# The ending of the last sequence pair moved into the slot that projects pair 0, and the first norm and small weight products into the last turn with heads or states

## What is computed

```
x = u
x = x + attn_a(layernorm(x), ...)   # selective state space block in chunk form (SSD)
x = x + ffn(layernorm(x), ...)      # two layers: local attention, then a gated feed forward
x = x + attn_b(layernorm(x), ...)   # a state scan over 256 steps, 16 states
x = x + ffn(layernorm(x), ...)      # the same two layers, the same weights
```

## Time and profile before

| | us |
|---|---|
| median of 3 runs | 2616.57 |
| lowest to highest | 2613.26 to 2620.62 |
| the profiled execution: its time | 2621.68 |
| the profiled execution: span of the trace | 2619.9 |
| TensorE busy | 2173.0 |
| VectorE busy | 1997.5 |
| ScalarE busy | 1836.2 |
| GpSimd busy | 1542.2 |

### The profile page before, as it was taken

One profiled execution on the slowest core, in us unless ns is written; L12 is line 12 of the kernel. 1 busy time (PEld: TensorE's weight loads), 2 busy tenths in 40 slices (PEclk: granted clock), 3 DMA queues, 4 the chain that ended last, 5 costly groups with the idle time before them and its releaser, 6 DMA issues. The chain is left out here.

```text
span 2619.9 us, 46190 instructions
## 1 busy us (share of the span) xinstructions
PE 2173.0 (83%) x13308; PEld 1114.0 (43%) x13308; DVE 1997.5 (76%) x5421; ACT 1836.2 (70%) x4729; POOL 1542.2 (59%) x1364
## 2 busy tenths in 40 slices
PE   5888689999999999666767667766799999999997
PEld 3555354555555555222222222222455555555553
DVE  4776477777777776389998999997777777777774
ACT  3444277777787777487787768875777777777774
POOL 1333275556565665176787777775756566665662
PEclk9998799999999999779899987989999999999999
DMA  3000000000000000000000000000000000000000
GB/s 130 1 0 1 5 18 9 14 13 9 13 14 13 12 9 14 0 0 1 1 1 1 0 1 1 0 0 1 14 17 10 12 14 10 13 18 21 17 14 17
DMA packets 12194, 29.92 MB, mean 11 GB/s; under 512 B 2240, under 2 KB 2240, under 8 KB 11584
## 3 DMA queue, kind: packets, MB, share of 16 engines
q1 hardware_dynamic: 11968, 27.41, 3.9%
HBM read 8.52 MB, written 2.10 MB: 4 GB/s over the span
## 5 line engine op out<-in xcount | busy, mean ns | idle before, releaser
L517 POOL TENSOR_TENSOR arena<-arena 128x512 f32<-128x512 f32 x256 | 325.1, 1270 | 447.0 <-DVE arena L1537 447.0
L573 POOL TENSOR_TENSOR arena<-arena 128x512 f32<-128x512 f32 x256 | 331.3, 1308 | 139.7 <-ACT arena L1262 137.2
L523 POOL TENSOR_TENSOR arena<-arena,SR 128x512 f32<-128x512 f32 x256 | 285.6, 1116 | 111.6 <-ACT SR L1144 110.7
L1617 DVE TENSOR_TENSOR_SCAN arena<-arena,psum 128x512 f32<-128x512 f32 x256 | 311.2, 1215 | 3.4
L935 PE MATMUL psum<-BS,tabs 96*128 96x512 bf16 x384 | 141.0, 424 | 194.0 <-DVE arena L1617 192.2
L1543 DVE TENSOR_REDUCE SM<-arena 128x8 f32<-128x512 f32 x256 | 175.6, 686 | 156.8 <-ACT arena L1134 143.8
L530 POOL TENSOR_TENSOR P<-P,RS 128x512 f32<-128x512 f32 x256 | 270.3, 1056 | 34.5 <-DVE RS L1464 34.1
L1003 PE MATMUL psum<-arena,first 128*128 128x512 f32 x512 | 288.7, 655 | 1.9 <-POOL arena L566 1.9
L1134 ACT ACTIVATE arena<-psum 128x512 f32<-128x512 f32 x256 | 151.6, 592 | 189.2 <-PE psum L859 187.9
L859 PE MATMUL psum<-rest,HA 128*128 128x512 f32 x512 | 270.4, 610 | 0.4 <-DVE HA L1452 0.4
L813 PE MATMUL psum<-HN,rest 128*128 128x512 f32 (+1 forms) x384 | 201.1, 651 | 56.1 <-ACT arena L1127 51.0
(11 more groups left out here) (221 smaller groups left out, 5237.4 us busy)
## 6 DMA issues: line engine op xcount, KB each, us to landing
arena<-arena SPq DMA_DIRECT2D x128, 128.0 KB, 2.3
rest<-in_rest SPq DMA_DIRECT2D x1, 4183.0 KB, 21.0
X<-in_x SPq DMA_DIRECT2D x1, 2048.0 KB, 9.0
out<-X SPq DMA_DIRECT2D x8, 256.0 KB, 2.3
tabs<-in_tabs SPq DMA_DIRECT2D x1, 1216.0 KB, 11.5
first<-in_first SPq DMA_DIRECT2D x1, 875.5 KB, 4.6
```

Source lines behind the costliest of these rows:

```text
L517: nc.gpsimd.tensor_tensor(CQ[:, n % 2, :], CQ[:, n % 2, :], SQN[:, n % 2, :], ALU.add).then_inc(f_rope, 1)
L523: nc.gpsimd.tensor_tensor(heads, heads, SR[:, n % 2, :].unsqueeze(2).to_broadcast([128, HEADS, DH]), ALU.mult).then_inc(f_qk, 1)
L573: nc.gpsimd.tensor_tensor(WU[:, k % DEEP, :], RG[:, k % DEEP, :], U[(t.j + pair) % 2][:, k % 2, :], ALU.mult).then_inc(m_wu, 1)
L1617: v.tensor_tensor_scan(HS[:, k % DEEP, :], AB[:, k % DEEP, :], B_BANK[k % 2], 0.0, ALU.mult, ALU.add).then_inc(m_hs, 1)
```

## The change

Four things are done, the arithmetic staying what it was.

1. Turn 8 is gone from both stages. VectorE still does its steps 0 and 1 right behind turn 7 (they finish the sum and gate it). The rest of pair 7's ending stands in slot -1, placed by tables from steps `h` of the slot to steps of the ending: `pe_closing`, `act_closing`, `dve_closing`. Its sums go to `CLOSE` (bank 1) in place of `STAT`.
2. The engines wait for `a_yd` and `m_g` (pair 7's sum is out of its banks) in place of `a_x` and `m_x` before the layers; `a_x` and `m_x` are waited for in slot -1 before the first scores.
3. Slot -2 is gone. Its contents, the first norm and shift of pair 0, stand in turn 7 (`t.final`) of each stage: in the scan the mean at `k` = 1, centring at 3, square at 5, variance at 7, root at 10, product and shift at 13.
4. The small weight products stand in turn 7 of the SSD stage: `small_sums` at steps 6 and 10 and the beta product at 11, the tables and biases on VectorE at 3, 5, 13 and 15.

```diff
+        CLOSE = bank[1]
...
         def passes(eng, ph, slot):
 
-            for n in (-2, -1, 0, 1):
+            for n in (-1, 0, 1):
                 slot(Slot(eng, ph, 0, n))
...
+                self.final = j == PAIRS - 1
+                self.stat = CLOSE if j == PAIRS else STAT
...
             turn(Turn(eng, 0, PAIRS - 1))
-            turn(Turn(eng, 0, PAIRS))
...
-            for j in range(PAIRS - 3, PAIRS + 1):
+            for j in range(PAIRS - 3, PAIRS):
                 turn(Turn(eng, 0, j))
...
+                    if t.final and q == 3:
+                        square_first(0)
...
+            staged(pool, pool_heads)
+            pool.wait_ge(a_yd, 2 * PAIRS)
             layers_pool(0)
...
+                    if t.final and k == 5:
+                        square_first(1)
...
+            def small_sums(l):
+                for g in range(2):
+                    for m, (at, size) in enumerate(HID_TILES):
+                        mm(X_BANK[1][0:size, 8 * l + 3 * g + m:8 * l + 3 * g + m + 1],
+                           W(f"w1{l}", HID * g + at, HID * g + at + size), W(f"lb{l}"), start=True, stop=True)
+
+            def a_pe_final(t, h):
+                first = Slot(pe, 0, 0, -2)
+                if h == 2:
+                    t.wait_ge(a_xt, 4, 4)
+                    pe.wait_ge(a_x, 1)
+                    outer_mean(first, X_BANK[0])
+                elif h in (6, 10):
+                    pe.wait_ge(in_rest, 16)
+                    small_sums((h - 6) // 4)
+                elif h == 8:
+                    outer_var(first, X_BANK[0])
+                elif h == 11:
+                    for k in range(2):
+                        last = mm(X_BANK[1][:, 16:17], W("b_wout", 128 * k, 128 * k + 128), W("b_beta", k, k + 1),
+                                  start=k == 0, stop=k == 1)
+                    last.then_inc(pre_ps, 1)
+
+            def pe_closing(k, h):
+                if k.ph:
+                    at = {3: 1, 4: 2, 8: 5, 9: 6, 15: 13, 16: 14}
+                    if h in at:
+                        pe_ending(Turn(pe, 0, PAIRS), at[h])
+                else:
+                    at = {5: 4, 6: 5, 13: 8, 14: 9}
+                    if h in at:
+                        a_pe_ending(Turn(pe, 0, PAIRS), at[h])
+
             def pe_dense(k, h):
+                if k.j == -1:
+                    pe_closing(k, h)
...
+                    if k.j == -1 and g == 6:
+                        pe.wait_ge(m_x if k.ph else a_x, PAIRS)
...
+                    if t.final and k == 1:
+                        t.wait_ge(m_zs, 2, 2)
+                        outer_mean(Slot(pe, 1, 0, -2), SIDE)
+                    if t.final and k == 7:
+                        outer_var(Slot(pe, 1, 0, -2), SIDE)
...
-            pe.wait_ge(m_x, PAIRS)
+            pe.wait_ge(m_g, 2 * PAIRS)
             layers_pe(1)
...
+            def act_closing(k, h):
+                if k.ph:
+                    at = {5: 7, 9: 10}
+                    if h in at:
+                        act_ending(Turn(act, 0, PAIRS), at[h])
+                else:
+                    at = {0: 2, 8: 6}
+                    if h in at:
+                        a_act_ending(Turn(act, 0, PAIRS), at[h])
...
+                    if t.final and k == 10:
+                        root_first(1, SIDE)
...
+            def a_dve_final(t, h):
+                if h == 3:
+                    dve.wait_ge(in_rest, 16)
+                    layer_tables(0)
+                elif h == 4:
+                    centre_first(0, X_BANK[0])
+                elif h == 5:
+                    layer_tables(1)
+                elif h == 12:
+                    normalise_first(0)
+                elif h == 13:
+                    dve.wait_ge(pre_ps, 1)
+                    layer_weights(0)
+                elif h == 15:
+                    layer_weights(1)
+                    scan_weights()
+                    scan_biases()
...
+            def dve_closing(k, h):
+                if k.ph:
+                    at = {4: (3, 4), 12: (9, 10), 18: (16,)}
+                    for step in at.get(h, ()):
+                        dve_ending(Turn(dve, 0, PAIRS), step)
+                else:
+                    at = {10: (7,), 16: (10,)}
+                    for step in at.get(h, ()):
+                        a_dve_ending(Turn(dve, 0, PAIRS), step)
...
+                    if t.final and k == 3:
+                        centre_first(1, SIDE)
+                    if t.final and k == 13:
+                        normalise_first(1)
 
             pairs(dve, dve_turn)
-            dve.wait_ge(m_x, PAIRS)
+            for k in (0, 1):
+                dve_ending(Turn(dve, 0, PAIRS), k)
+            dve.wait_ge(m_g, 2 * PAIRS)
             layers_dve(1)
```

133 lines of the change are left out of this document (74 added, 59 removed).

## The result

| | median us | runs | ratio to before, 95% interval |
|---|---|---|---|
| before, first comparison | 2617.32 (2606.47 to 2627.86) | 11 | |
| after, first comparison | 2599.87 (2594.40 to 2606.07) | 11 | 0.9935 [0.9921, 0.9948] |
| after, once more (below) | 2599.25 (2594.95 to 2603.96) | 6 | 0.9914 [0.9897, 0.9931] |

A forecast was written before the change was run, and what follows sets the result against it. No engine is full; chains of waits at the two stage ends bound the kernel. Net savings of 18.3 us (SSD seam) and 7.5 us (scan seam), 25.8 together, off the median of 2616.6 gave 2591 us, range 2581 to 2605.

The forecast's parts named there:

- Seam 1 (a): Behind the SSD stage: the mean of pair 1 still stands alone ahead of the first projection, costing 1.0 us.
- Seam 1 (b): SSD turn 7 grows by 8.4 us: one-column passes 5.7, variance 1.0, mean 1.7; bounds 6.7 and 14.4.
- I give it nothing: SSD turn 7: GpSimd's square queued ahead of head 4's decays was taken to cost 0 us.
- has no room: End of SSD turn 7: TensorE idles only 0.5 of 9.55 us, so its added matmuls count in full.
- Seam 1 (c): Pair 7's ending inside slot -1 behind the SSD stage costs 2.0 us; bounds 0 and 8.5.
- Seam 2 (b): Scan turn 7 grows by 3.8 us from VectorE's added work and a stall behind ScalarE's root; bounds 2.2 and 6.1.
- Seam 2 (c): Pair 7's ending inside slot -1 behind the scan costs 5.3 us; bounds 2.0 and 9.6.
- B: Rival: slot -1 grows by the whole ending, 10.7 and 9.6 us; gain 12.8, time 2604; chance 0.18.
- C: Rival: last turns and slot -1 absorb nearly all added work; gain 34.4 us, time 2582; chance 0.10.
- E: Rival: most work only moves, upper bounds throughout; gain 6.7 us, time 2610; chance 0.05.
- D: Rival: TensorE's clock stays at 1.2 GHz through slots -1 and 0; 13.4 us slower, 2630; chance 0.03.
- theory B of experiment 1: The change lengthens layers and scan between the seams; with the SSD seam alone, trace loses 5 to 7 us.

The follow-up runs named there:

- experiment 1: Two kernels, each with the change at one seam, the other seam as before: SSD seam alone 2605.25 us (0.9949 to before), scan seam alone 2611.26 us (0.9972).
- the repetition: The changed kernel unaltered, run and profiled once more: 2599.25 us, ratio 0.9914 to the kernel before.
- `seam_ssd_only`: The changed kernel with the old end of the scan kept, so only the seam behind the SSD stage is changed: 2605.25 us, ratio 0.9949 to before.
- edits 3 and 4: Changed kernel with GpSimd's first-norm square behind head 5's decays, not head 3's, and the small weight products moved to SSD turn -1: together 2598.82 us.
- experiment 2: Changed kernel without the rest of pair 7's ending in slot -1, in both stages: 2586.87 us, ratio 0.9881 to before.
- experiment 5: Changed kernel with both halves of the ending's variance ahead of item 0's transposes in slot -1 behind the scan: 2598.66 us, ratio 0.9919 to before.
- `sq_prod_act`: Changed kernel with edits 3 and 4, and ScalarE instead of VectorE making the layers' first shift, in scan turn 7: 2593.44 us, ratio 0.9894 to before.

## Why the prediction was right, and where it was off

**What was removed** stands: 29.7 and 17.6 us became 1.92 and 1.02, and TensorE and VectorE, then idle, had the same work elsewhere. That each comes out as time is shown by experiment 1 (13 and 7 us); that seam 1 brings more than seam 2 has the medians for it, while the intervals of the two overlap.

**Seam 1 (a)**, 1.0 against 1.92: mis-sized. I took the matmul at full clock. The row at 283.79 has 2.08, behind an idle time of 2.02, at a clock of 0.51 (2.07, 2.02 and 0.50 in the repetition). Where the clock was 1.00, in `seam_ssd_only`, the stretch was 1.02.

**Seam 1 (b)**, 8.4 against 8.53 and 5.53: right in sum, wrong in its making. The passes were priced from rows at 285 to 291 us, where the granted clock was 0.50, and came out at 4.1 in place of 5.7, in the repetition, all at full clock, at 3.1. My upper bound of 14.4 took these slow rows times 1.8 once more, and is too high for that. That VectorE's added work "lies beside TensorE's" failed as well: it is 5.0 to 7.1 us, and once the wait and the passes are out of the way TensorE stands 2.5 us for it. "I give it nothing", of the square in GpSimd's queue, is the step that failed: my reason was that TensorE gets to head 4 only behind the previous pair's sums, and it got there 2.6 us too early. Against a turn at full clock (16.27) the growth is 5 us with edits 3 and 4 and 7.8 to 11.6 without, and of these the wait is part. So that the sum came out at 8.53 is in part luck: the yardstick of 19.22 was 3 us long by its clock, and the missing wait made up for passes priced too high. That TensorE "has no room" held only for the last 9.55 us.

**Seam 1 (c)**, 2.0 against 2.37 and 3.59, and 2.3 or 3.6 by experiment 2: right for the first profile, low for the second.

**Seam 2 (b)**, 3.8 against 5.24 and 4.96: mis-sized, by 1.0 for product and shifts and by 0.3 for the stall. I had put the short times at about half. The rule of the Trainium skill, page "SBUF — State Buffer", section "Who interferes with whom", by which the three would have taken 4.1 and the sum 24.3, was nearer: 3.6 were measured, with both shifts blocked.

**Seam 2 (c)**, 5.3 against 6.53 and 8.98: mis-sized. The two places at which I had it late were right to 0.3 us (4.84 for 5.0, 4.8 for 4.5 late). Experiment 2 has 4.7 to 7.2 for the ending. Without the ending the slot is 1.8 longer than the slot of before, whose first norm of pair 1 had begun ahead of its first projection; I hadn't priced this, but it lies inside the scatter and was not tried. In the repetition this slot ran at a clock of 0.83, and has 2.4 more.

**The rivals.** B needed waits of over 3 us that move the ring. They are there behind the scan: 3.65 us of ScalarE on the variance, in the repetition 4.43, and there 3.56 of VectorE behind the root (2.79 in after). In experiment 5 ScalarE's is lifted, and 0.2 us of that is left at item 2. The ending took 7.0 to 10.7 us in both slots, not 20.3. So B's mechanism fell, although its 2604 lies nearer to the first comparison's 2599.9 than my 2591 does; its gain of 12.8 lies outside that comparison's interval (13.6 to 20.7), if barely. C and E fell with their gains of 34.4 and 6.7 us, outside both comparisons. D fell: slots -1 ran at 0.84 and 0.86. The clock does take part, but in the stretches named above.

**What stays open.** The seams give 18 to 22 us in the traces and the time 17.4 and 23.1; which is right between these can't be told, as the identical stretch between the seams scatters from 1394 to 1411 us. Nor is it shown why. A rival is left here, theory B of experiment 1, and my own sign of being wrong, a stage far from the seams that changes its length. The stretch lasted 1401.1 and 1401.8 us in the two profiles with the old SSD seam; in the eleven with the new one 1405.7 to 1411.3 seven times and 1393.7 to 1402.2 four times. That is scatter on both sides of the old length, with more of it above. Its mean granted clock was 0.923 in the longest and 0.935 in the shortest, so the clock may carry part of it.

## What to carry to other kernels

Work taken from an idle seam must be priced in the place it goes to: TensorE's time at the clock of that place, VectorE's time beside GpSimd, and each in-order queue that it enters, above all where it waits in that queue for another engine ahead of work that a third one needs. A piece of a few tenths to 2 us in front of the producer of a loop's next input costs its wait and not its length; put it behind the next one or two of these (here this took the wait away, and no time that could be measured). When one profile of the kernel before serves as the yardstick, look at the granted clock of the stretch first: the same turn here took 16.3 or 19.2 us. And a piece can merely change its place, as the small products at the start did.

The best complete kernel here is `sq_prod_act`: the change, with edits 3, 4 and 6, at 2593.44 us. It is not shown to beat the changed kernel beyond its interval.
